# Flamingo gated block, one core: score products and masks cut into four column tiles of 32 keys instead of two of 64

## What is computed

```python
x = x + jnp.tanh(g_xattn[0]) * mha(_layernorm(x), ctx_2048, ctx_2048)
x = x + jnp.tanh(g_ffn[0]) * ffn(_layernorm(x), w_gate, w_up, w_down, ...)

# mha, per head: S = 512 queries, SK = 1601 keys, hd = 32
scores = einsum('bhqd,bhkd->bhqk', qh, kh) / sqrt(hd)
scores = where(ki <= qi + (Sk - Sq), scores, -10000.0)
out    = einsum('bhqk,bhkd->bhqd', softmax(scores), vh)

# ffn: per-row scale, round to fp8, product with rounded weights
qx = fp8(x / scale_x)
g, u = qlinear(qx, w_gate), qlinear(qx, w_up)
t = silu(g) * u
y = qlinear(fp8(t / scale_t), w_down)
```

## Time and profile before

| | before |
|---|---|
| median of 2 runs | 1158.63 us |
| lowest to highest | 1156.97 to 1160.3 us |
| the profiled execution | 1161.19 us |
| its span on the core | 1159.4 us |
| mean granted TensorE clock | 0.949 of full speed |
| matmuls (PE) / weight loads (PEld) | 7770 / 7770 |
| DMA, mean | 61 GB/s |

### The profile page before, as it was taken

One profiled execution on the slowest core, in us unless ns is written; L12 is line 12 of the kernel. 1 busy time (PEld: TensorE's weight loads), 2 busy tenths in 40 slices (PEclk: granted clock), 3 DMA queues, 4 the chain that ended last, 5 costly groups with the idle time before them and its releaser, 6 DMA issues.

```text
span 1159.4 us, 21085 instructions
## 1 busy us (share of the span) xinstructions
PE 970.5 (84%) x7770; PEld 399.4 (34%) x7770; DVE 859.7 (74%) x1438; ACT 656.5 (57%) x1343; POOL 332.1 (29%) x350
## 2 busy tenths in 40 slices
PE   4588889888879989999889999998899999984344
PEld 2233333333323334343334333333333343432222
DVE  7768789887747888777677877787778786446764
ACT  2165567675646666666556666665566666753321
POOL 3012323332101414132323232222314132443343
PEclk9998899999989999999999999999999999996766
DMA  7942423230572221114812121218421110000000
GB/s 147 154 122 69 115 66 93 66 86 26 112 88 57 66 57 39 53 43 83 124 41 60 63 61 36 51 41 115 70 61 35 27 41 10 2 10 10 10 10 19
DMA packets 155119, 70.69 MB, mean 61 GB/s; under 512 B 111032, under 2 KB 142856, under 8 KB 155016
## 3 DMA queue, kind: packets, MB, share of 16 engines
q1 hardware_dynamic: 153256, 63.57, 26.5%
q0 software_dynamic: 1760, 5.77, 1.8%
HBM read 39.08 MB, written 4.19 MB: 37 GB/s over the span
## 4 chain that ended last, share of the span: by engine, by line
PE 42%; DVE 36%; issue 10%; ACT 4%; POOL 4%; DMA 2%; SPq 1%; POOLq 0%; DVEq 0%; ACTq 0%
DVE mch L1069 17%; PE ps L866 13%; PE ps L842 8%; PE ps L887 6%; PE ps L780 5%; PE ps L910 3%; DVE ff L985 2%; DVE ff L981 2%; DVE ff L989 2%; PE ps L785 2%; ACT pr L632 1%; DVE upd L1112 1%; DMA qst<-mrow 1%; PE ps L848 1%; DVE cmb L1102 1%
## 5 line engine op out<-in xcount | busy, mean ns | idle before, releaser
L632 ACT ACTIVATE pr<-ps 128x512 f32<-128x512 f32 (+4 forms) x832 | 397.2, 530 | 250.0 <-PE ps L842 125.1
L1069 DVE TENSOR_REDUCE mch<-ps 128x2 f32<-128x1024 f32 (+4 forms) x416 | 432.3, 1056 | 69.2 <-PE ps L780 32.8
L866 PE MATMUL ps<-pr,vf 128*33 128x512 f32 (+4 forms) x1664 | 380.6, 537 | 0.0
L842 PE MATMUL ps<-qst,kst 97*64 97x512 f16 (+4 forms) x1600 | 250.5, 371 | 18.0 <-DMA qst<-mrow 11.4
L780 PE MATMUL ps<-kTh,qTh 32*128 32x512 f16 (+4 forms) x832 | 156.2, 373 | 59.2 <-DVE mch L1069 40.7
L780 PEld LDWEIGHTS ps<-kTh,qTh 32*128 32x128 f16 x832 | 39.5, 92 | 279.0 <-DVE mch L1069 106.9
L842 PEld LDWEIGHTS ps<-qst,kst 97*64 97x64 f16 (+1 forms) x1600 | 77.3, 111 | 108.0 <-ACT pr L632 57.4
L866 PEld LDWEIGHTS ps<-pr,vf 128*33 128x33 f32 (+1 forms) x1664 | 86.8, 113 | 56.6 <-issue 4.9
L1141 DVE SCALAR_TENSOR_TENSOR ff<-ps,scs,wsb 128x352 f32<-128x352 f32 x56 | 32.6, 583 | 73.1 <-PE ps L887 73.1
L448 POOL TENSOR_TENSOR t_q<-ff 128x768 bf16<-128x768 f32 (+1 forms) x28 | 47.4, 1694 | 100.1 <-DVE ff L989 100.1
L887 PE MATMUL ps<-wgu,t_T 128*64 128x352 bf16 x768 | 66.5, 316 | 0.0
(11 more groups left out here) (151 smaller groups left out, 1198.2 us busy)
## 6 DMA issues: line engine op xcount, KB each, us to landing
kst<-kTh SPq DMA_DIRECT2D x128, 100.1 KB, 2.2
ksrc<-in_ctx SPq DMA_DIRECT2D x16, 768.0 KB
vf<-in_ctx SPq DMA_DIRECT2D x48, 256.0 KB, 5.1
kst<-kTl SPq DMA_DIRECT2D x64, 100.1 KB, 2.2
xs<-in_x SPq DMA_DIRECT2D x16, 256.0 KB, 4.8
qst<-qTh SPq DMA_DIRECT2D x128, 32.0 KB, 1.9
out<-xs SPq DMA_DIRECT2D x16, 256.0 KB, 2.0
ff<-in_L_ffn_w_down SPq DMA_DIRECT2D x4, 704.0 KB, 4.4
```

Source lines behind the costliest of these rows:

```text
L632: nc.scalar.activation(pr[0:kn, n % NP, q0:S], ps[0:kn, j, q0:S], ACT.Exp, scale=SCALE).then_inc(ex_done, 1)
L842: last = nc.tensor.matmul(ps[a:e, j, q0:S], kst[s][0:ST, r, k0 + a:k0 + e], qst[s][0:ST, r, q0:S], start=True, stop=(t < DT))
L866: nc.tensor.matmul(ps[64 * j:64 * j + VW, 2 + pp % 2, q0:S], vf[0:kn, t, h, :], pr[0:kn, n % NP, q0:S], start=(t == 0), stop=(t == NT - 1) ...
L1069: nc.vector.tensor_reduce(mch[:, qt, 2 * hp:2 * hp + 2, c], both[:, :, 0:k1 - k0], AX.X, ALU.max).then_inc(dve_free, 1)
```

## The change

The 128 keys of a tile are cut into four pieces of 32 columns in place of two of 64, in the score product and in the mask that is added to it. The last key tile of 65 keys, which was one piece, becomes pieces of 32, 32 and 1 column. The products with row maxima, the value products and the feed-forward block keep their shapes. No wait, no semaphore, no DMA and no instruction of another engine changes. The last piece still signals `qk_mm`.

```diff
+    QUARTERS = tuple((P // 4 * i, P // 4 * (i + 1)) for i in range(4))
...
-            halves = HALVES if kn == P else [(0, kn)]
+            quarters = [(a, min(e, kn)) for a, e in QUARTERS if a < kn]
...
-                for a, e in halves:
+                for a, e in quarters:
                     last = nc.tensor.matmul(ps[a:e, j, q0:S], kst[s][0:ST, r, k0 + a:k0 + e], qst[s][0:ST, r, q0:S],
                                             start=True, stop=(t < DT))
...
-                    for a, e in halves:
+                    for a, e in quarters:
                         last = nc.tensor.matmul(ps[a:e, j, q0:q0 + n_m], idb[:, a:e], maskT[:, m0:m0 + n_m], start=False, stop=True)
```

## The result

The changed kernel took 1188.72 us (median of two runs, 1187.63 and 1189.8), 30 us more than the median before of 1158.63: a ratio of 1.0266 with a 95% interval of 1.0227 to 1.0306. Run again with other kernels, it had 1189.27 us against 1160.46, ratio 1.0232 (1.0204 to 1.026).

The account below looks back on a forecast made before the run. The prediction saw TensorE and VectorE taking turns as the bound, DMA far off. Streaming and instructions at 0, shape changes 30 + 8 = +38 us on the profiled 1161.19 us gave 1199, 1197 us for the median; range 1183 to 1225.

Parts of the forecast that it names:

- No more streaming time: Score and mask products on TensorE: four pieces side by side stream in the time of two, cost 0.
- The rival of 165 us: Score products: four pieces don't run side by side, 165 us more on TensorE, 1330 us and more; chance 2%.
- Instructions at 0: TensorE: 2304 more matmuls and as many loads lie under the streaming and cost 0.
- A change of shape costs 0.12 us: TensorE, between stationary tile shapes: about 0.10 us at the change, plus 0.02 to 0.03 for the first load behind it.
- the rival that it costs nothing: TensorE: going between 32 and 64 columns is free, 1156 to 1159 us; chance 5%.
- 509 new changes: TensorE's instruction order: shape changes go from 1003 to 1512, 61 us if each showed in full.
- The sign behind the 4-column transposes (L795): Scores behind these transposes: 15 changes of shape fewer, 14 of them on the chain, if the transposes count as 32.
- Where TensorE waits: TensorE's wait for its PSUM slot at L780, 360 to 960 us: 54.8 us, 69 times, for VectorE's L1069.
- the second rival: Steps shared with VectorE: VectorE hides most, under 23 us show, 1160 to 1181 us; chance 8%.
- What of it shows: 251 on the chain, none of them hidden, plus a quarter of the rest: Chain from 60 to 1040 us: 251 changes cost 30 us; of the other 258 (31 us), 8 us show.
- The sum of 38 us: Whole kernel: 30 us from changes on the chain plus 8 us from the others, +38 us.
- Shorter loads give nothing: Weight loads of 32 columns in place of 64: gain 0, as mean load times were 113 and 111 ns.

Follow-up runs that it names:

- 1536 pairs: Kernel before, each 64-column score product cut in two along the queries, no new change of shape: 1162.5 us against 1158.74, ratio 1.0026.
- 1153: Changed kernel with each value product's 33 columns cut into 32 and 1: 1170.14 us, ratio to before 1.0089.
- 1363: Changed kernel with the mask on the maxima also in four pieces of 32 columns: 1181.35 us, ratio to before 1.0173.
- 1512: The changed kernel itself, against the kernel before: 1188.72 us; run again 1189.27 us.
- 1522: Kernel before with a tile's 128 keys in one piece of 128 columns, score and mask: 1189.88 us against 1158.74, ratio 1.026.
- the paired maxima: Kernel before with the maxima products of two steps issued together: 1205.89 us with masks behind both, 1203.07 us with each mask behind its own product.
- the twelve steps: Kernel before with 32-key pieces only in steps 3 to 9 and 16 to 20 of each group: 1173.66 us against 1158.74, ratio 1.0157.
- the 14 steps: Kernel before with 32-key pieces only in steps 21 to 25, 0 to 2 and 10 to 15 of each group: 1180.79 us, ratio 1.0211.

## Why the prediction was right, point by point

- **No more streaming time.** Right. The timeline after and that of the values in 32 and 1 columns show four pieces side by side, in f16 and in f32. The rival of 165 us is out.
- **Instructions at 0.** Nearly right: 1536 pairs cost 1 to 5 us, so the 2304 would be 1 to 8 us. The forecast took 0; the interval excludes 0 narrowly.
- **A change of shape costs 0.12 us.** Right: 0.10 at the change and 0.02 behind it, for 32 to 64 columns as for 128 to 64; and TensorE's busy time grew by 0.10 us for each. That 32 is a shape of its own was inferred; the rival that it costs nothing is out. The Trainium skill, "TensorEngine Tiling (Array Packing)", key properties, says that a change of tiling mode drains the array. The traces agree in that each change has a gap, of 0.10 us; they don't show a drain itself.
- **509 new changes.** Right in effect: kernels with 1153, 1363, 1512 and 1522 changes, whose numbers of matmuls run the other way in part, took 10, 21, 29 and 31 us more than the kernel before beside them, some 0.06 us for each change. The sign behind the 4-column transposes (L795) was right too, see below.
- **Where TensorE waits.** Misread in one row. The 54.8 us at L780 in the earlier trace rows are idle time of the weight loads (PEld), part of it while matmuls still ran. TensorE's matmul side waited there 21 times for 19.4 us (the row shown with the paired maxima). So the gaps in which new cost could hide were smaller than the text has it for the second rival, though their sum, 42 of 600 us, was read rightly.
- **What of it shows: 251 on the chain, none of them hidden, plus a quarter of the rest.** This was the weak step. The sum of 38 us was too large by about a quarter; it measured 30. That 251 x 0.12 = 30 is also the measured value is luck, because the split behind it was wrong. If all of the 251 showed, nothing would be left for the other 258, yet the kernel that changed only the twelve steps, with some 15% of the 251 (under 5 us at 0.12), took 15 us more. And in the 14 steps, where by the chain at least three quarters of the cost should show, the traces have 50 to 60%. So "these can't be hidden" failed, and of the rest more than nothing showed; how the 30 us divide between the two stays open, since the whole times and the traces divide them differently. The mechanism of the second rival, that a part is hidden in the gaps, was at work, with less force than it needed: about half of the 61 us showed.
- **Shorter loads give nothing.** Nearly right. The load of 32 columns is shorter in the trace, 98 ns for a mask where 64 columns take 111, so a load does get shorter with fewer columns, though the prediction's two means didn't show it. The Trainium skill, "TensorE: Matmul & The Clock Gate", section on LDWEIGHTS, has load time in proportion to the columns, and by it the difference is 27 ns; the trace agrees in the direction and has half the size, 13 ns. It hardly counts where loads are hidden.

The loads of the changed kernel (columns as in the earlier trace rows):

```profile
L849 PEld LDWEIGHTS ps<-maskT,idb 128*32 128x32 bf16 x1152 | 35.0, 98 | 0.0
L786 PEld LDWEIGHTS ps<-idb,maskT 128*64 128x64 bf16 x640 | 23.4, 111 | 24.9 <-issue 16.4
```

## What to carry to other kernels

Count the places where TensorE goes from one tile shape to another, since each takes 0.12 us of it here. The shape goes by ranges of the stationary operand's size: 33 columns ran as 64 did, 1 and 4 as 32 did, while 65 columns were apart from 64, and 32 rows from 97. Keep neighbouring products in one shape even if that means more pieces. Cutting finer costs next to nothing by itself (1536 pieces more took 1 to 5 us), and cutting one product of a sequence alone is what costs. What of such a cost shows can't be read from the chain as yes or no: here about half showed, 50 to 60% in the traces where TensorE was mostly on it and 28 to 36% where it mostly wasn't. So a bound from both sides and a kernel that changes only some steps are worth more than the count. A comparison of single traces over a part of the span was good to some 3 us here, and its shares moved with the part that was chosen.

## What the runs showed of the hardware that was not expected

The scores behind the 4-column transposes of the maxima (L795) start while the transposes still run, once both have the 32-column shape. In the changed kernel:

```profile
503.98 0.27 PE L795 MATMUL ps<-idh,m 128*4 128x128 f16 x2 [0.37 <-DVE ff L1142]
504.05 0.32 PE L843 MATMUL ps<-qst,kst 97*32 97x321 f16 x3
504.09 0.27 PE L795 MATMUL ps<-idh,m 128*4 128x128 f16 x2
504.19 0.23 PE L849 MATMUL ps<-maskT,idb 128*32 128x128 bf16 x3
504.20 0.36 PE L843 MATMUL ps<-qst,kst 97*32 97x321 f16 x4
...
504.69 1.05 PE L867 MATMUL ps<-pr,vf 128*33 128x512 f32 x4
```

And before:

```profile
496.76 0.38 PE L794 MATMUL ps<-idh,m 128*4 128x128 f16 x4 [0.37 <-DVE ff L1141]
497.07 0.33 PE L842 MATMUL ps<-qst,kst 97*64 97x321 f16 x2
...
497.49 1.02 PE L866 MATMUL ps<-pr,vf 128*33 128x512 f32 x4
```

Three of the four score pieces start at 504.05, beside the transposes that use only the first column range, and run 0.15 us ahead of the fourth, which starts at 504.20. By the kernel's addresses the fourth shares its column range with the transposes and has to come after them. Pieces in different column ranges go on independently here, also when they belong to different products, while the shape stays. Before, with 64 columns behind 4, the scores started 0.31 us after the first transpose, behind all four of them and the change of shape. From the first transpose to the values it is 0.71 us now and was 0.73, although the values now stand behind a new change of shape. So some 0.1 us is won here, about the 0.12 us that the sum had, and the early start of three pieces wins no more than that. This happens once a group, in 15 of the 16 groups.
